# Joining two 256-column weights into one 512-column moving operand in a software-pipelined four-layer graph kernel, with a new hand-written order on every engine

## The chip, the cores and the metric

The kernel runs on one core of one Trainium2 chip. The metric is device time in microseconds (us), from start to end of one execution; the time before is the median of three runs. A core has five engines that work side by side, each through its own list of instructions in the order in which the program wrote them: TensorE (PE: matmuls, which write to PSUM banks; its weight loads, PEld, overlap the matmuls), VectorE (DVE), ScalarE (ACT), GpSimd (POOL) and SyncE (SP, which issues the DMAs). They wait for one another only through semaphores.

## The reference

32 graphs of 256 nodes with 256 features pass through four layers, each with a residual sum and a normalisation (mean and variance over the features). Layers A and D are masked attention with 4 heads of 64, G is a gated graph layer with 4 heads, B an attention with 8 heads of 32 that is also cut by a cosine threshold.

```python
# A, D: attention over the neighbours
attn = softmax(where(adj, q @ k.T / sqrt(64), -big));  y = (attn @ v) @ Wo + bo
# G, h = the node features, for each of 4 heads:
Wh  = h @ W[head].T + bW[head]
A_mat = tanh(where(adj, (Wh @ attn[head]) @ Wh.T, 0))
hp  = relu(A_mat @ Wh)
ha  = concat(hp over heads) @ A_w.T;   hf = h @ fc_w.T
c   = sigmoid(hf @ g1_w.T + ha @ g2_w.T + gbias);   y = hf * c + ha * (1 - c)
# B, 8 heads of 32:
m   = embs @ map_w.T + map_b
n   = m / |m| per head;  cos_adj = (n @ n.T masked) > 0.1
p   = softmax(where(masked, -big, q(m) @ k(m).T / sqrt(32)))
sem_h = embs @ gcn_map_w.T + gcn_map_b;   adj = cos_adj * p
y   = relu((adj @ sem_h) @ gcn_W.T / (adj.sum(-1) + 1))
```

## The kernel before

**Stages and order.** The work on one graph in one layer is cut into stages with names such as `g_wh_0` (layer G, node vectors Wh of head 0), `b_m` (layer B, the product m) or `d_x_t` (layer D, transpose of its input). A step of the program runs one stage list per engine, in which each stage carries the number of steps that its graph lags behind; layers A, G, B and D of up to four graphs are so interleaved. The lists are written out by hand in the tables ORDER (the loop body: 27 iterations, one graph enters and one leaves in each), FILL and DRAIN (ahead of the loop and behind it). Nothing reorders them later: what stands in a table is what the engine does next.

**Products.** float32 values are kept as a high and a low part, and `pe_product` issues three matmuls for each product: high by high, high by low (lines 462 and 463, the same weights) and low by high (464), each with 128 rows of weights and, in the node-major stages, 256 moving columns. `pe_node_major` does so for two halves of the nodes (`it`) and two halves of the features (`kc`): 12 matmuls a stage. `g_wh_h` is one such stage for each of the four heads, into the bank BA[1]; `b_m` and `b_sem` are two more, into BB[1] and BB[0].

**Around the two chains that the prediction speaks of.** In layer B the PE stage `b_out` (line 451, four transposes with `ident,b`) is followed on DVE by `b_scale` (1801), `b_sum` (1805) and `b_stats` (373 and 378), on POOL by `b_rstd` (393 and 395), on DVE by `b_norm_out` (385, two instructions, x from SBUF to SBUF), and then on PE by `d_x_t` (451, `ident,x`). DVE's next stages behind `b_norm_out` are `g_ha_t` (630), for which the PE stage `g_gate` waits, and `g_diff` (1688). While that chain runs PE does the stages `g_ha_h_nt` (six matmuls each), `g_hf`, `g_ha_t` and `g_gate_x`. POOL's stages there are `b_mask` (1882: the uint8 adjacency becomes an additive mask) and `g_x_ha` (1869: a sum of two float32 tiles, all in SBUF). Between A and G the PE stages `b_m`, `b_k`, `b_q` stand ahead of `g_x_t` (451, `ident,a`), which waits for DVE's `a_norm_out` (385); DVE's stage `b_m` (1764, adds the bias) stands just ahead of that. In layer B the PE stages `b_transpose_n` (1420) wait for DVE's `b_cut_n` (1733), which need ACT's `b_exps_n` (1571).

Of the kernel before, what the change touches and what calls it, by code (L numbers as in the profile page):

```python
# [731 lines left out]
def build(nc, d, out_dram):  # L732

    with ExitStack() as ctx:
# [1203 lines left out]
```

## Time and profile before

| | |
|---|---|
| median of 3 runs | 2638.91 us (2637.47 to 2639.14) |
| span of the profiled execution, first to last instruction | 2634.6 us |
| own time of that execution | about 2639 us (its span and some 4 us around it) |
| granted PE clock, mean of the span | 0.989 of full speed |
| PE busy | 2561.4 us, 97% (22,097 matmuls) |
| DVE, ACT, POOL busy | 76%, 54%, 35% |
| loop of 27 iterations | about 334 to 2450 us |

Busy time is the time in which an engine has an instruction in work; matmuls are pipelined, so a matmul's listed duration is longer than the distance to the next one's start, and that distance (the pace) is what counts in a stream. In a row of the timeline the bracket behind an instruction gives how long its engine sat idle ahead of it, and what ended the wait.

### The profile page before, as it was taken

To read this page: it belongs to the slowest core of one execution; us is meant where nothing else is said; L and a number is where in the kernel's file an instruction comes from. 1 tells how busy PE (TensorE), PEld (TensorE's weight loads), DVE (VectorE), ACT (ScalarE), POOL (GpSimd) and SP (SyncE) were. 2 spreads that over 40 slices of the span, in tenths; PEclk is the share of its full clock that TensorE was granted. 3 is DMA by queue.
4 is the path that set the end of the run, shared out by engine and by line. 5 is a ranking of instruction groups with operands and counts; after the bars stand their busy time and mean duration, and the time that the engine had idled before them with its cause. 6 is when DMAs were issued, how large, how long until landed. Compare 5 with 4: busy or idle time off the path is not lost.

```text
span 2634.6 us, 63306 instructions
## 1 busy us (share of the span) xinstructions
PE 2561.4 (97%) x22097; PEld 2293.3 (87%) x22097; DVE 2006.3 (76%) x6629; ACT 1409.9 (54%) x3925; POOL 917.0 (35%) x988
## 2 busy tenths in 40 slices
PE   7999999999999999999999999999999999999985
PEld 7888888898888899888889888889888889888874
DVE  3577877777877787877887787787787787787764
ACT  2355555655654555555565555565565555565442
POOL 3233333343333344333334333334333334433330
PEclk9999999999999999999999999999999999999997
DMA  4000000000000000000000000000000000000000
GB/s 135 7 1 12 11 11 0 10 10 10 10 10 9 1 10 10 10 10 9 1 10 10 10 10 10 0 10 10 10 10 10 4 6 10 10 10 0 11 6 9
DMA packets 44490, 29.90 MB, mean 11 GB/s; under 512 B 21264, under 2 KB 44048, under 8 KB 44432
## 3 DMA queue, kind: packets, MB, share of 16 engines
q1 hardware_dynamic: 44432, 29.13, 3.8%
q8 instruction: 35, 0.57, 0.1%
q14 instruction: 23, 0.19, 0.0%
HBM read 20.73 MB, written 8.39 MB: 11 GB/s over the span
## 4 chain that ended last, share of the span: by engine, by line
PE 84%; ACT 5%; DVE 2%; issue 1%; POOL 0%; ACTq 0%; DVEq 0%; POOLq 0%
PE bank L462 21%; PE bank L464 19%; PE bank L463 19%; PE bank L1420 4%; ACT arena L594 4%; PE bank L519 4%; PE bank L528 3%; PE bank L451 3%; PE bank L1411 3%; PE bank L539 3%; PE bank L1402 2%; PE bank L1430 2%; DVE arena L678 1%; PE bank L1244 1%; DVE b L635 0%
## 5 line engine op out<-in xcount | busy, mean ns | idle before, releaser
L393 POOL TENSOR_SCALAR l_ve<-l_mv 128x2 f32<-128x2 f32 x128 | 28.8, 225 | 1022.2 <-DVE l_mv L378 1021.9
L1571 ACT ACTIVATE b<-b,s_sh 128x256 f32<-128x256 f32 x512 | 254.8, 503 | 97.4 <-DVE s_sh L635 97.4
L462 PE MATMUL bank<-arena_r 128*128 128x256 f32 x1024 | 303.1, 296 | 0.2
L464 PE MATMUL bank<-arena_r 128*128 128x256 f32 x1024 | 289.1, 282 | 0.0
L463 PE MATMUL bank<-arena_r 128*128 128x256 f32 x1024 | 289.0, 282 | 0.0
L1836 POOL TENSOR_TENSOR arena_r<-a,arena_r 128x512 fp32r<-128x512 f32 x128 | 165.5, 1293 | 335.8 <-ACT arena_r L1508 335.7
L1831 POOL TENSOR_TENSOR arena_r<-a,arena_r 128x512 fp32r<-128x512 f32 x128 | 166.7, 1303 | 165.9 <-ACT arena_r L1514 165.9
L1733 DVE SCALAR_TENSOR_TENSOR b<-bank,b 128x256 f32<-128x256 f32 x512 | 191.0, 420 | 36.0 <-ACT b L1571 27.6
L462 PEld LDWEIGHTS bank<-arena_r 128*128 128x128 f32 x1024 | 194.7, 190 | 21.4 <-issue 21.2
L635 DVE CUSTOM_DVE_ANT_0 b<-bank,s_add 128x256 f32<-128x256 f32 x512 | 181.5, 420 | 23.9 <-PE bank L1402 14.8
L463 PEld LDWEIGHTS bank<-arena_r 128*128 128x128 f32 x1024 | 195.2, 191 | 0.0
L464 PEld LDWEIGHTS bank<-arena_r 128*128 128x128 f32 x1024 | 194.8, 190 | 0.0
L1638 DVE SCALAR_TENSOR_TENSOR arena_r<-bank,g_b_z,arena_r 128x256 fp32r<-128x256 f32 x256 | 112.2, 480 | 90.5 <-ACT arena_r L1489 89.6
L594 ACT ACTIVATE b<-b,l_sh 128x256 f32<-128x256 f32 x256 | 126.7, 497 | 85.0 <-DVE l_sh L635 85.0
L462 PE MATMUL bank<-g_w_a_hi,arena_r 128*128 128x256 f32 x512 | 155.0, 303 | 0.0
L462 PE MATMUL bank<-g_w_t_hi,arena_r 128*128 128x256 f32 x512 | 150.8, 295 | 1.5 <-DVE arena_r L630 1.5
L462 PE MATMUL bank<-arena_r,g_w_z_hi 128*128 128x256 f32 x512 | 147.0, 287 | 1.6 <-DVE arena_r L630 1.6
L463 PE MATMUL bank<-arena_r,g_w_z_hi 128*128 128x256 f32 x512 | 143.8, 281 | 0.0
L464 PE MATMUL bank<-arena_r,g_w_z_lo 128*128 128x256 f32 x512 | 143.7, 281 | 0.0
L464 PE MATMUL bank<-g_w_a_hi,arena_r 128*128 128x256 f32 x512 | 143.0, 279 | 0.0
L463 PE MATMUL bank<-g_w_t_lo,arena_r 128*128 128x256 f32 x512 | 142.9, 279 | 0.0
L464 PE MATMUL bank<-g_w_t_hi,arena_r 128*128 128x256 f32 x512 | 142.9, 279 | 0.0
(280 smaller groups left out, 9041.7 us busy)
## 6 DMA issues: line engine op xcount, KB each, us to landing
x_in<-in_x SPq DMA_DIRECT2D x32, 256.0 KB, 2.8
out<-x SPq DMA_DIRECT2D x32, 256.0 KB, 2.1
adj_a<-in_adj SPq DMA_DIRECT2D x32, 64.0 KB, 2.5
adj_b<-in_adj SPq DMA_DIRECT2D x32, 64.0 KB, 1.8
a<-in_L_gnn_W SPq DMA_DIRECT2D x4, 256.0 KB, 3.3
b<-in_L_gnn_A_w SPq DMA_DIRECT2D x1, 1024.0 KB, 7.6
arena<-in_L_gnn_attn SPq DMA_DIRECT2D x4, 256.0 KB, 7.2
g_b_wh<-in_L_gnn_bW SPq DMA_DIRECT2D x1, 512.0 KB, 9.2
```

The source lines that it names most:

```text
L462: pe.matmul(out, w[0], x[0], start=first, stop=False)
L463: pe.matmul(out, w[0], x[1], start=False, stop=False)
L464: return pe.matmul(out, w[1], x[0], start=False, stop=last)
L519: last = pe.matmul(B[2 * pair + half][:, it * NODES:(it + 1) * NODES], L.qt[rows, pair, it * P:(it + 1) * P], L.kt[rows, pair, :], start=T ...
L594: last = act.activation(L.e[:, h, it, :], L.e[:, h, it, :], ACT.Exp, bias=L.sh[:, h, it:it + 1], scale=-1.0, accum_out=L.sums[:, h, it:it ...
L635: return dve.tensor_tensor_reduce(out, scores, add, -scale, ceiling, ALU.add, ALU.min, lowest)
L1420: last = pe.transpose(BB[n][:, jt * NODES + it * P:jt * NODES + (it + 1) * P], S.e[:, n, it, jt * P:(jt + 1) * P], C.ident[:, :])
L1571: last = act.activation(S.e[:, n, it, :], S.e[:, n, it, :], ACT.Exp, bias=S.sh[:, it, h:h + 1], scale=-1.0, accum_out=S.sums[:, it, h:h + 1])
L1638: last = dve.scalar_tensor_tensor(G.zt[h % 2][1][:, dt, :], BA[0][:, dt * NODES:(dt + 1) * NODES], G.b_z[:, dt, h:h + 1], G.zt[h % 2][0][: ...
L1733: last = dve.scalar_tensor_tensor(S.e[:, n, it, :], BB[n][:, it * NODES:(it + 1) * NODES], COS_MIN, S.e[:, n, it, :], ALU.is_gt, ALU.mult, ...
L1831: pool.tensor_tensor(G.wh[h % 2][1], G.whf[:, h % 2, :, :], G.wh[h % 2][0].bitcast(F32), ALU.subtract).then_inc(G.wh_sb.sem, 1)
L1836: pool.tensor_tensor(G.am[h % 2][1], G.th[:, h % 2, :, :], G.am[h % 2][0].bitcast(F32), ALU.subtract).then_inc(G.a.sem, 1)
```

## The change

The weights of two heads of `g_wh` are kept side by side (`G.w_t_pair`, 512 columns), and so are those of `b_m` and `b_sem` (`S.w_ms`). A new helper, `pe_node_rows`, multiplies one half of the nodes by all 512 columns and fills a whole bank: the stage `g_wh_h` now computes node half h % 2 for the head pair h // 2, with 6 matmuls of 512 columns for 12 of 256; `b_m` computes m and sem for both node halves, with 12 of 512 for 24 of 256, into BB[0] and BB[1], and PE's stage `b_sem` is gone. DVE adds the bias to the two heads in one instruction of 512 elements for each `g_wh` stage. ACT's and POOL's parts of head 0 now need both stages of the pair. Some waits are added (PE's `b_m` for `D.o_sb`, `b_unit_t` for `S.sem_sb`; ACT's `g_a` for `G.p_psum`; two of SP's loads). All tables are written anew; the loop body also begins at another stage.

```diff
+def pe_node_rows(pe, out, x_t, w, it):
+
+    for kc in range(T):
+        last = pe_product(pe, out, part(x_t, slice(None), kc, slice(it * P, (it + 1) * P)), part(w, slice(None), kc),
+                          kc == 0, kc == T - 1)
+    return last
...
-                pe_node_major(pe, BA[1], G.xt, G.w_t[h]).then_inc(G.wh_psum.sem, 1)
+                pe_node_rows(pe, BA[1][:, :], G.xt, G.w_t_pair[h // 2], h % 2).then_inc(G.wh_psum.sem, 1)
...
-                pe_node_major(pe, BB[1], S.xt, S.w_m).then_inc(S.m_psum.sem, 1)
+                    pe.wait_ge(D.o_sb.sem, D.o_sb.all(g - 1))
+                for it in range(T):
+                    last = pe_node_rows(pe, BB[it][:, :], S.xt, S.w_ms, it)
+                last.then_inc(S.m_psum.sem, 1)
...
-            def b_sem(g):
-                pe.wait_ge(S.x_t_sb.sem, S.x_t_sb.at(g))
-                if later(g):
-                    pe.wait_ge(D.o_sb.sem, D.o_sb.all(g - 1))
-                pe_node_major(pe, BB[0], S.xt, S.w_s).then_inc(S.sem_psum.sem, 1)
...
             def b_unit_t(g):
                 pe.wait_ge(S.unit.sem, S.unit.at(g))
+                pe.wait_ge(S.sem_sb.sem, S.sem_sb.at(g))
...
             def g_wh(g, h):
-                act.wait_ge(G.wh_f.sem, G.wh_f.at(g, h + 1))
+                act.wait_ge(G.wh_f.sem, G.wh_f.at(g, h - h % 2 + 2))
...
             def g_wh(g, h):
+                pair, it = h // 2, h % 2
                 dve.wait_ge(G.wh_psum.sem, G.wh_psum.at(g, h + 1))
-                if h >= 2:
-                    dve.wait_ge(G.wh_sb.sem, G.wh_sb.at(g, h - 1))
-                for it in range(T):
-                    last = dve.tensor_tensor(G.whf[:, h % 2, it, :], BA[1][:, it * DIM:(it + 1) * DIM],
-                                             G.b_wh[:, h * DIM:(h + 1) * DIM], ALU.add)
-                last.then_inc(G.wh_f.sem, 1)
+                if pair:
+                    dve.wait_ge(G.wh_sb.sem, G.wh_sb.at(g, 2))
+                dve.tensor_tensor(G.whf[:, :, it, :], view(BA[1]),
+                                  G.b_wh[:, 2 * pair * DIM:(2 * pair + 2) * DIM].rearrange("p (h n) -> p h n", n=DIM),
+                                  ALU.add).then_inc(G.wh_f.sem, 1)
```

The tables put other neighbours around these stages. The order of PE in the loop body around `b_out` was this; `g_w_a1` to `g_w_a3` are the weights of the `g_ha` stages, one stage for each change of weights or bank (three rows, then three more), and the row with `b32` is `b_out`:

```order
L464 MATMUL bank2<-g_w_a1_hi,arena_r_50 128x256
L1435 ISA
L451 MATMUL bank4<-ident,b32 128x128 x4
L462 MATMUL bank2<-g_w_a2_hi,arena_r_50 128x256
L463 MATMUL bank2<-g_w_a2_lo,arena_r_50 128x256
L464 MATMUL bank2<-g_w_a2_hi,arena_r_50 128x256
```

and is now this, still on PE:

```order
L465 MATMUL bank2<-g_w_a1_hi,arena_r_50 128x256
L1452 REGISTER_ALU
L452 MATMUL bank4<-ident,b32 128x128 x4
L463 MATMUL bank2<-g_w_a3_hi,arena_r_50 128x256
L464 MATMUL bank2<-g_w_a3_lo,arena_r_50 128x256
L465 MATMUL bank2<-g_w_a3_hi,arena_r_50 128x256
```

The stage `g_ha_2_1` (weights `g_w_a2`) stood behind `b_out` and stands two stages ahead of it now: behind `b_out` come `g_ha_3_1`, `g_ha_3_0`, `g_hf`, `g_ha_t`, `g_gate_x`, `d_x_t` and `g_gate`, as before but for that one. On POOL the rows from `b_sums` (`s_sd`) on, with `b_rstd` (`l2_ve`, `l2_rs`), were these:

```order
L1901 TENSOR_TENSOR s_sd<-s_sums,s_drop 128x16
L393 TENSOR_SCALAR l2_ve<-l2_mv 128x2
L395 TENSOR_TENSOR l2_rs<-l2_ve,minus_half 128x2
L1878 ISA
L1882 TENSOR_SCALAR s_add<-adj_b 128x512
L1869 TENSOR_TENSOR a32<-a32 128x512
L728 TENSOR_TENSOR x3<-x3,l3_bo 128x256 x2
```

and are now, on POOL again:

```order
L394 TENSOR_SCALAR l2_ve<-l2_mv 128x2
L396 TENSOR_TENSOR l2_rs<-l2_ve,minus_half 128x2
L1882 REGISTER_ALU
L1886 TENSOR_TENSOR a32<-a32 128x512
L1870 ISA
L1874 CAST g_adj_bf<-adj_a 128x512
L742 TENSOR_TENSOR a32<-x_in,l0_bo 128x256 x2
L742 TENSOR_TENSOR x3<-x3,l3_bo 128x256 x2
```

`g_x_ha` (`a32<-a32`) stands right behind `b_rstd` where `b_mask` (`s_add`) stood; six stages now stand between `b_rstd` and `b_mask`. On DVE the rows around the first `b_cut` (`b,s_dsum<-bank,b`) were these, at the end of the loop body before:

```order
L1647 TENSOR_TENSOR a<-a,g_adj_t 128x512
L1638 SCALAR_TENSOR_TENSOR arena_r<-bank,g_b_z,arena_r 128x256 x2
L1731 ISA
L1733 SCALAR_TENSOR_TENSOR b,s_dsum<-bank,b 128x256 x2
L1731 REGISTER_ALU
L1733 SCALAR_TENSOR_TENSOR b,s_dsum<-bank,b 128x256 x2
```

and are now, on DVE, where the row `x<-x,l_mv,l_rs` is `d_norm_out`:

```order
L1655 SCALAR_TENSOR_TENSOR arena_r<-bank,g_b_z,arena_r 128x256 x2
L1748 ISA
L1750 SCALAR_TENSOR_TENSOR b,s_dsum<-bank,b 128x256 x2
L386 TENSOR_SCALAR x<-x,l_mv,l_rs 128x256 x2
L1748 REGISTER_ALU
L1750 SCALAR_TENSOR_TENSOR b,s_dsum<-bank,b 128x256 x2
```

`d_norm_out` moved from a place ahead of all four masks to one between the first two cuts. In the same table `g_c_t` and `g_z_1` moved behind `b_mask_0`, and `g_diff` moved ahead of `b_norm_out`. On PE `b_k` moved from between `b_m` and `b_q` to a place behind `g_x_t`.

## Rows read from the trace of the kernel before

**Rows 1.** The page: head and first line of the busy times (its part 1).

```profile
span 2634.6 us, 63306 instructions
PE 2561.4 (97%) x22097; PEld 2293.3 (87%) x22097; DVE 2006.3 (76%) x6629; ACT 1409.9 (54%) x3925; POOL 917.0 (35%) x988
```

**Rows 2.** Busy time by stretch; columns named in the first line.

```profile
core 0: us, PE busy (x) PEld busy (x) DVE busy (x) ACT busy (x) POOL busy (x), PEclk, DMA share, GB/s
330.00:2450.00 2120.00, 2110.21 (x18456) 1892.42 (x18459) 1678.49 (x5575) 1178.59 (x3301) 759.96 (x812) 1.00 0.03 8
76.00:81.00 5.00, 4.91 (x23) 4.58 (x24) 1.10 (x4) 1.30 (x3) 0.00 (x0) 0.50 0.00 0
```

**Rows 3.** Timeline (start, duration, engine, line, instruction, [idle before]) of DVE, one iteration apart.

```profile
1277.40 0.69 DVE L1801 TENSOR_TENSOR x<-bank,s_fac 128x512 f32<-128x512 f32 x1 [1.85 <-PE bank L451]
...
1355.76 0.69 DVE L1801 TENSOR_TENSOR x<-bank,s_fac 128x512 f32<-128x512 f32 x1 [1.85 <-PE bank L451]
```

**Rows 4.** Timeline of PE: from `b_m` to `g_x_t`, first matmul of each stage.

```profile
1231.71 0.28 PE L462 MATMUL bank<-s_w_m_hi,b32r 128*128 128x256 f32 x1
...
1233.13 0.28 PE L462 MATMUL bank<-b32r,s_w_k_hi 128*128 128x256 f32 x1
...
1234.58 0.28 PE L462 MATMUL bank<-b32r,s_w_q_hi 128*128 128x256 f32 x1
...
1236.01 0.60 PE L451 MATMUL bank<-ident,a 128*128 128x128 f32 x4
```

**Rows 5.** Timeline of PE in the fill, two neighbours of a `g_wh` stage.

```profile
80.10 0.41 PE L464 MATMUL bank<-g_w_t_hi,arena_r 128*128 128x256 f32 x1
80.31 0.41 PE L462 MATMUL bank<-g_w_t_hi,arena_r 128*128 128x256 f32 x1
```

**Rows 6.** Timeline of PE: `b_out`, the two `g_ha` stages behind it, `d_x_t`, `g_gate`.

```profile
1276.65 0.60 PE L451 MATMUL bank<-ident,b 128*128 128x128 f32 x4
...
1277.80 0.28 PE L462 MATMUL bank<-g_w_a_hi,arena_r 128*128 128x256 f32 x1
...
1278.50 0.28 PE L462 MATMUL bank<-g_w_a_hi,arena_r 128*128 128x256 f32 x1
...
1282.48 0.60 PE L451 MATMUL bank<-ident,x 128*128 128x128 f32 x4
1282.97 0.39 PE L462 MATMUL bank<-g_w_g_hi,arena_r 128*128 128x256 f32 x1
```

**Rows 7.** Timeline of DVE in that stretch: `b_norm_out`, `g_ha_t`.

```profile
1281.19 1.13 DVE L385 TENSOR_SCALAR x<-x,l_mv,l_rs 128x256 f32<-128x256 f32 x2 [1.24 <-POOL l_rs L395]
1282.24 0.68 DVE L630 TENSOR_TENSOR arena_r<-bank,arena_r 128x512 fp32r<-128x512 f32 x1
```

**Rows 8.** Timeline of POOL in that stretch: `b_mask`, `g_x_ha`.

```profile
1281.24 1.54 POOL L1882 TENSOR_SCALAR s_add<-adj_b 128x512 bf16<-128x512 uint8 x1
1282.76 1.28 POOL L1869 TENSOR_TENSOR a<-a 128x512 f32<-128x512 f32 x1
```

**Rows 9.** Timelines of DVE and POOL at one `d_norm_out`, near the loop's end.

```profile
2445.19 1.71 DVE L385 TENSOR_SCALAR x<-x,l_mv,l_rs 128x256 f32<-128x256 f32 x2
...
2444.07 1.30 POOL L1836 TENSOR_TENSOR arena_r<-a,arena_r 128x512 fp32r<-128x512 f32 x1 [2.28 <-ACT arena_r L1508]
2445.33 1.43 POOL L1831 TENSOR_TENSOR arena_r<-a,arena_r 128x512 fp32r<-128x512 f32 x1
```

**Rows 10.** Timeline of DVE: bias add of `b_m`, then `a_norm_out`.

```profile
1233.72 0.72 DVE L1764 TENSOR_TENSOR b<-bank,s_b_m 128x256 f32<-128x256 f32 x2
1235.03 0.74 DVE L385 TENSOR_SCALAR a<-a,l_mv,l_rs 128x256 f32<-128x256 f32 x2 [0.59 <-POOL l_rs L395]
```

**Rows 11.** Timelines of DVE (`d_norm_out`, end of the last of four cuts) and PE (`b_transpose_2`, `_3`).

```profile
1243.32 0.73 DVE L385 TENSOR_SCALAR x<-x,l_mv,l_rs 128x256 f32<-128x256 f32 x2
...
1256.67 0.42 DVE L1733 SCALAR_TENSOR_TENSOR b<-bank,b 128x256 f32<-128x256 f32 x1
...
1256.97 1.03 PE L1420 MATMUL bank<-ident,b 128*128 128x128 f32 x8
```

More of the change, by code:

```diff
@@ L110 @@
-        ("a_q", 1), ("a_v", 1), ("a_scores_0", 1), ("b_x_t", 0), ("a_scores_1", 1), ("b_m", 0), ("b_k", 0),
-        ("a_probs_0", 1), ("a_probs_1", 1), ("a_probs_2", 1), ("a_probs_3", 1), ("a_values_0", 1), ("a_values_1", 1),
-        ("b_q", 0), ("a_out", 1), ("b_sem", 0), ("g_adj_t", 1), ("b_unit_t", 0), ("b_scores_0", 0), ("g_x_t", 1),
[7 rows of a table removed]
-        ("g_ha_t", 1), ("a_x_t", 2), ("d_q", 0), ("g_gate_x", 1), ("d_scores_0", 0), ("g_gate", 1), ("d_v", 0),
[3 rows of a table removed]
-        ("a_out", 2), ("d_out", 0), ("b_sem", 1), ("b_m", 1), ("g_x_t", 2), ("b_q", 1), ("b_k", 1), ("g_c", 2),
[7 rows of a table removed]
@@ new lines @@
+        ("a_q", 1), ("a_v", 1), ("b_x_t", 0), ("a_scores_0", 1), ("a_scores_1", 1), ("b_q", 0), ("b_m", 0),
+        ("a_probs_0", 1), ("a_probs_1", 1), ("a_probs_2", 1), ("a_probs_3", 1), ("a_values_0", 1), ("a_values_1", 1),
+        ("b_k", 0), ("a_out", 1), ("b_unit_t", 0), ("g_x_t", 1), ("b_scores_0", 0), ("g_adj_t", 1), ("g_wh_0", 1),
[6 rows of a table added]
+        ("g_ha_3_1", 1), ("g_hf", 1), ("d_x_t", 0), ("g_ha_t", 1), ("a_x_t", 2), ("g_gate_x", 1), ("g_gate", 1),
+        ("d_k", 0), ("d_q", 0), ("d_v", 0), ("a_k", 2), ("d_scores_0", 0), ("d_scores_1", 0), ("a_q", 2), ("a_v", 2),
@@ L144 @@
+        ("g_gate", 2), ("d_q", 1), ("d_k", 1),
     ],
@@ L182 @@
-        ("b_stats", 0), ("g_p_3", 1), ("b_norm_out", 0), ("d_x_t", 0), ("g_diff", 1), ("a_x_t", 2), ("g_ha_t", 1),
-        ("d_mask_0", 0), ("g_gate", 1), ("d_mask_1", 0), ("d_v", 0), ("g_mix", 1), ("g_sum", 1), ("d_norm_p_0", 0),
[3 rows of a table removed]
-        ("b_x_t", 1), ("a_sum", 2), ("a_stats", 2), ("d_sum", 0), ("a_norm_out", 2), ("b_m", 1), ("b_square", 1),
-        ("g_x_t", 2), ("b_sem", 1), ("d_stats", 0), ("b_unit", 1), ("g_z_0", 2), ("g_c_t", 2), ("g_wh_0", 2),
-        ("g_adj_t", 2), ("g_z_1", 2), ("b_mask_0", 1), ("b_mask_1", 1), ("b_mask_2", 1), ("b_mask_3", 1),
@@ new lines @@
+        ("g_z_3", 0), ("g_wh_3", 0), ("g_p_1", 0), ("g_a_3", 0), ("g_p_2", 0), ("g_p_3", 0), ("g_ha_t", 0),
+        ("g_diff", 0), ("g_gate", 0), ("a_x_t", 1), ("g_mix", 0), ("g_sum", 0), ("g_stats", 0), ("g_norm_out", 0),
+        ("a_v", 1), ("b_x_t", 0), ("a_mask_0", 1), ("a_mask_1", 1), ("a_mask_2", 1), ("a_mask_3", 1),
+        ("a_norm_p_0", 1), ("a_norm_p_1", 1), ("a_probs_1", 1), ("a_probs_3", 1), ("b_m", 0), ("b_square", 0),
+        ("a_o_copy", 1), ("b_sem", 0), ("a_sum", 1), ("a_stats", 1), ("b_unit", 0), ("a_norm_out", 1), ("g_x_t", 1),
[6 rows of a table added]
@@ L191 @@
+        ("b_stats", 0), ("g_p_3", 1), ("b_norm_out", 0), ("g_diff", 1), ("g_ha_t", 1), ("a_x_t", 2), ("d_x_t", 0),
+        ("g_gate", 1), ("g_mix", 1), ("g_sum", 1), ("g_stats", 1), ("d_v", 0), ("d_mask_0", 0), ("d_mask_1", 0),
[3 rows of a table added]
+        ("d_sum", 0), ("b_x_t", 1), ("a_sum", 2), ("a_stats", 2), ("b_m", 1), ("a_norm_out", 2), ("b_square", 1),
+        ("g_x_t", 2), ("d_stats", 0), ("g_adj_t", 2), ("b_sem", 1), ("g_wh_0", 2), ("b_unit", 1), ("g_z_0", 2),
[4 rows of a table added]
     ],
     "POOL": [
-        ("b_keep", 0), ("a_bias", 0), ("a_mask", 0), ("g_adj", 0), ("d_mask", 0), ("w_d", 0), ("a_rstd", 0),
@@ L221 @@
-        ("b_m", 0), ("b_sem", 0), ("b_k", 0), ("b_q", 0), ("b_unit_t", 0), ("b_scores_0", 0), ("b_cos_0", 0),
-        ("b_transpose_0", 0), ("b_transpose_1", 0), ("b_transpose_2", 0), ("b_transpose_3", 0), ("b_values_0", 0),
-        ("b_scores_1", 0), ("b_cos_1", 0), ("b_transpose_4", 0), ("b_transpose_5", 0), ("b_transpose_6", 0),
-        ("b_transpose_7", 0), ("b_values_1", 0), ("b_out", 0), ("d_x_t", 0), ("d_q", 0), ("d_k", 0), ("d_v", 0),
-        ("d_scores_0", 0), ("d_scores_1", 0), ("d_probs_0", 0), ("d_probs_1", 0), ("d_probs_2", 0), ("d_probs_3", 0),
@@ new lines @@
+        ("g_x_t", 1), ("g_wh_0", 1), ("b_sem", 2), ("b_unit", 2), ("g_c_t", 1), ("g_z_0", 1), ("g_z_1", 1),
[5 rows of a table added]
+        ("b_copy_7", 2), ("g_p_3", 1), ("b_factors", 2), ("b_scale", 2), ("b_sum", 2), ("b_stats", 2), ("g_diff", 1),
+        ("b_norm_out", 2), ("g_ha_t", 1), ("d_x_t", 2), ("g_gate", 1), ("g_mix", 1), ("g_sum", 1), ("g_stats", 1),
[3 rows of a table added]
+        ("a_probs_1", 0), ("a_probs_3", 0), ("d_o_copy", 2), ("b_x_t", 1), ("a_o_copy", 0), ("d_sum", 2),
+        ("d_stats", 2), ("a_sum", 0), ("a_stats", 0), ("b_m", 1), ("a_norm_out", 0), ("b_square", 1), ("g_x_t", 0),
```

207 lines of the change are left out of this document (108 added, 99 removed), and 225 rows, old and new, of tables (DRAIN, FILL, ORDER).

## The prediction, made before the changed kernel was run

> **What bounds the kernel now.** I read the page first. PE is busy for 2561.4 of 2634.6 us [rows 1], so the question is whether the stream of matmuls ever stops. The busy times by stretch answer it: in the loop PE is busy for 2110.21 of 2120.00 us, at a granted clock of 1.00, which is the 2.4 GHz level [rows 2]. The loop is bound by PE; DVE and the others set the time only where PE reaches an instruction before its input is there. The timeline gives the period: the same DVE instruction comes again after 78.36 us [rows 3], and 27 iterations make some 2,115 us. So each 0.1 us that PE gains or loses in an iteration is 2.7 us at the end, and 0.2% (5.3 us), about what a measurement of this kernel can tell from no change, is 0.2 us an iteration.
>
> The sum is made against the profiled execution's own time, about 2639 us, which is the median of the runs to within a microsecond.
>
> **Term 1, the wide matmuls.** Per graph, four `g_wh` stages lose 6 matmuls each and `b_m` with `b_sem` loses 12: 36 pairs of 256 columns become 36 matmuls of 512, with the same columns in all. At full clock 12 matmuls of `b_m` take 1.42 us, from 1231.71 to 1233.13 [rows 4], 118 ns each; over the `g_wh` stages it is 114 to 118, and I take 117.5, so a pair costs 235 ns. The trace has no 512-column matmul of this kind, so it is bounded. At the half clock (0.50, the 1.2 GHz level [rows 2]) the same 256 columns come every 210 ns [rows 5], a column a cycle and nothing more. The upper bound is therefore twice today's pace, 235 ns, no gain; the lower is 512 columns at 2.4 GHz, 213 ns. If the 10 ns that today's pace has over 107 are paid once an instruction it is 224. Since nothing of the surcharge shows at the half clock, I take 219: 36 x 16 ns = **0.58 us saved** per graph, between 0 and 0.77.
>
> The Trainium skill, "TensorE: Matmul & The Clock Gate", section "Back-to-back issue gap", prices an isolated matmul at 109 ns for 256 columns and 216 for 512. The trace disagrees with its first figure (118). By both its figures the saving would be 36 x 2.5 ns, 0.09 us a graph; with its second figure and the row it would be 0.7. The same section gives 131 ns for 512 columns in a sustained stream; by that the saving would be 36 x 104 ns, 3.7 us a graph, and with the terms below the kernel would take about 2566 us. Rows 5 speak against it, since there the time follows the columns.
>
> PE is the bound, so this gain counts in full, if no new wait eats it. DVE's four saved instructions a graph count for nothing: DVE is busy for 79% of the loop [rows 2] and PE does not wait for its bias adds; they are hidden under PE's other stages.
>
> **Term 2, `b_out` to `g_gate`.** This place decides. From `b_out`'s end DVE and POOL run a fixed chain: scale, sum, statistics, POOL's `b_rstd`, `b_norm_out`, then `g_ha_t`; PE does other work meanwhile. Today the chain and the cover end together: PE starts `d_x_t` at 1282.48 and `g_gate` at 1282.97 [rows 6], and DVE ends `b_norm_out` at 1282.32 and `g_ha_t` at 1282.92 [rows 7]. PE's cover has about 0.1 us to spare at `d_x_t` and none at `g_gate`. In the change one `g_ha` stage, 0.70 us (1277.80 to 1278.50 [rows 6]), stands ahead of `b_out` instead of behind it. The chain is not shortened: `g_diff` moves ahead of `b_norm_out`, into DVE's idle 1.24 us there [rows 7], but `g_ha_t` still stands behind `b_norm_out`. So `g_gate` starts as long after `b_out` as before, with 0.70 us less work in between: **+0.70 us**. The stage that moved ahead covers nothing there, for PE did not wait at `b_out`.
>
> Then the chain may grow. `b_norm_out` takes 1.13 us for two instructions while POOL's `b_mask` starts 0.05 us behind it [rows 7, 8]; the same two instructions take 0.73 to 0.74 elsewhere [rows 10, 11]. One `d_norm_out` took 1.71: it began at 2445.19, POOL's sum of two SBUF tiles at 2445.33, and DVE's pair ended about when POOL did, at 2446.76 to 2446.90 [rows 9]. In the change POOL's instruction right behind `b_rstd` is `g_x_ha`, of the kind of rows 9 and 1.28 us long [rows 8]; it needs `g_ha`, long done by then. Its start falls against `b_norm_out` as in rows 9: first instruction 0.4 us, second held until POOL ends, 0.05 + 1.28 + 0.4 = 1.73 us or less. Bounds are 0.73 (no contact, -0.40 against today) and 1.73 (+0.60); I take 1.69, by the row it is nearest to: **+0.56**.
>
> The Trainium skill, "SBUF — State Buffer", section "🔬 SBUF: two separate sides", says that DVE and GpSimd share a port pair as an exclusive lock, held by whichever starts first for its whole instruction. Rows 9 agree for two-input sums; `b_mask` cost 0.40 rather than its whole 1.54.
>
> **Term 3, `g_x_t`.** PE reaches `g_x_t` 4.30 us behind the start of `b_m` today [rows 4], 0.24 after `a_norm_out` ends (1235.77 [rows 10]), of which some 0.05 is the signal. In the change the wide `b_m` (12 x 0.219 = 2.63) and `b_q` (1.43 [rows 4]) stand ahead: 4.06. But DVE's bias add for `b_m` is queued ahead of `a_norm_out` and now waits for the whole wide stage: 1231.71 + 2.63 + 0.1 for the signal + 0.72 = 1235.16, then `a_norm_out` to 1235.90, while PE is there at 1235.77. **+0.2 us**, between 0.1 and 0.3.
>
> **Term 4, the first four transposes.** `b_transpose_2` starts at 1256.97 and `_3` some 0.4 later, the last cut ends at 1257.09 [rows 11]: 0.25 us to spare. The change puts `d_norm_out` (0.73 [rows 11]) and two gated-layer stages between `b_mask_0` and the last cut, where DVE has idle time but no more than about as much. PE's distance from `b_scores_0` to these transposes is the same (`g_s_2` came ahead of them, `g_p_0` went behind). Between nothing and 0.5; I take **+0.25**.
>
> The moved `b_k`, `a_v` and `d_probs` lie beside work that does not wait for them; the added waits are for stages that end a layer earlier: nothing. The two SP waits hold the adjacency loads until the masks are made, one graph ahead of use: nothing either.
>
> **Sum** per iteration: -0.58 + 0.70 + 0.56 + 0.2 + 0.25 = **+1.13 us**, times 27: +30.5. In the fill and drain five graphs save 3 us and meet the same neighbours at `b_out`, about as much again: 0. Forecast **2670 us**; own range 2655 to 2685.
>
> **The rivals.**
> *`g_x_ha` does not meet `b_norm_out`* (it starts late, or DVE's pair goes first): the stretch stays at 1.13. For it: `b_mask` starts at the same point and costs only 0.40. Against: rows 9. -0.58 + 0.70 + 0.2 + 0.25 = 0.57, 2654 us. 0.22.
> *Faster.* `b_norm_out` at its bare 0.73, because `b_mask` is gone from its side, and wide matmuls near 215 ns (-0.72): term 2 falls to 0.30, terms 3 and 4 to 0.1 each: -0.22, 2633 us. The point that decides is `b_norm_out` below 0.9 us. For it: 0.73 wherever POOL is quiet. Against: POOL is not quiet there. 0.15.
> *`d_norm_out` is held as well.* It now sits among cuts, where POOL runs its two-input sums back to back, as in rows 9: 1 us more against 0.25 to spare, +0.75 on the forecast, 2690 us. For it: just such a place in rows 9. Against: DVE's idle time ahead of the cuts may absorb it. 0.15.
> *Columns faster than one a cycle*: 131 ns a wide matmul, -3.74 + 1.71 an iteration, 27 times, and five graphs of -3.7 outside the loop: 2566 us. Rows 5 speak against it; 0.01. It is the sustained figure of the Trainium skill quoted above.
>
> **How the numbers follow.** The forecast has 0.47. Range 2636 to 2693: it takes in the second rival's case and the third's and leaves out most of the faster one. Faster: 0.15 and 0.01 make 0.16; within 0.2%: the edge between the no-contact case and the faster one, 0.05; slower 0.79.
>
> **What would show it.** Wide matmuls starting every 219 ns (213 to 235); `g_gate`'s first matmul idle 0.7 us or more, released by `g_ha_t` on DVE; `b_norm_out` near 1.7 us beside a 1.28 us `g_x_ha`; `g_x_t` idle 0.2 behind `a_norm_out`; `b_transpose` idle behind a cut; a period near 79.5 us. I am wrong if the period is below 78.4, above all if PE does not wait at `g_gate` although a stage less covers the chain, or if `b_norm_out` is short.

## The result and the profile after

The changed kernel takes 2715.57 us (median of 4 runs, 2712.48 to 2716.89) against 2638.68 before: a ratio of 1.0297, 95% interval 1.0285 to 1.0309. It is 77 us slower; the forecast was 2670 and the range ended at 2693. The profiled execution has a span of 2714.4 us, 79.8 more than [rows 1]. That is 3 us more than the medians differ by: wherever a run here lists both, an execution takes some 1.9 us more than its span, so the profiled execution of before took about 2636.5 us, 2 us under the median, and not the 2639 that the prediction set its sum against.

The page of the changed kernel, its head and first line of busy times:

```profile
span 2714.4 us, 60943 instructions
PE 2592.9 (96%) x20945; PEld 2235.0 (82%) x20945; DVE 2015.2 (74%) x6501; ACT 1411.5 (52%) x3925; POOL 919.0 (34%) x988
```

There are 1152 matmuls fewer, 36 for each of 32 graphs, and PE is busy for 31.5 us *more*: a matmul counts to its modelled end, so busy time is not work done. The busy times by stretch of the changed kernel (columns as in [rows 2]) show it in the loop's steady part:

```profile
350.00:2440.00 2090.00, 2038.36 (x16701) 1756.60 (x16700) 1613.38 (x5231) 1129.30 (x3161) 733.01 (x780) 1.00 0.03 8
```

PE now stands idle for 2.5% of it, at the same granted clock; before it was 0.5% [rows 2]. The timeline of DVE in the changed kernel gives the period, 80.73 us for 78.36 [rows 3]:

```profile
1317.41 0.69 DVE L1818 TENSOR_TENSOR x<-bank,s_fac 128x512 f32<-128x512 f32 x1 [1.85 <-PE bank L452]
...
1398.14 0.69 DVE L1818 TENSOR_TENSOR x<-bank,s_fac 128x512 f32<-128x512 f32 x1 [1.84 <-PE bank L452]
```

The loop and its ends (the fill ahead of it, the drain behind it) can be taken apart. `b_out` of the second graph starts at 258.54 us before and 266.43 after; 27 graphs later it starts at 2373.42 and 2447.79. So the 27 periods cost 66.5 us, 2.46 each; the fill cost 7.9 and the drain 5.4.

To see which stage the 2.46 us are in, I took the distance from each PE stage's first matmul to that of the next stage, as the median over 17 graphs of the loop. They sum to 78.38 us before and 80.81 after. These are the stages that changed by over 0.2 us, with the two that stand behind such a one or lost matmuls (`d_x_t`, `g_wh`) and with `b_sem`, which is gone. A wait counts for the stage ahead of it:

```
stage (next stage)                 before   after
g_gate_x (d_x_t)                     1.50    2.95
d_x_t (g_gate)                       0.50    0.60
b_m and b_sem                        2.94    2.81
b_q (after: g_x_t)                   1.44    1.65
b_transpose_1 (after: _2)            0.36    0.79
b_transpose_2 (_3)                   0.43    0.69
a_probs_1                            0.98    0.47
d_values_0                           0.91    1.42
g_wh_0 to g_wh_3, sum                5.95    5.91
```

The wait at `a_probs_1` only moved to `d_values_0`. What is left of the loop's 2.43 us is +1.56 at `d_x_t` and `g_gate`, +0.28 at `g_x_t` (0.06 of it in the next stage), +0.74 at the transposes (0.06 in the third), -0.17 from the wide matmuls: 2.41 in all.

**The place at `d_x_t`.** In this place PE covers a chain on DVE and POOL: it does other work (the cover) while the chain runs, and waits if the cover ends first. The waits of PE for a normalisation (`x`) and for the cuts (`b`), as the profile sums them, for the kernel before and then for the changed one (us in total, times, longest):

```profile
PE bank L451 <- DVE x L385: 4.6, 1, 4.6
PE bank L1420 <- DVE b L1733: 2.1, 3, 0.9
```

```profile
PE bank L452 <- DVE x L386: 42.8, 31, 4.6
PE bank L1437 <- DVE b L1750: 7.4, 31, 0.9
```

One wait for a normalisation became 31, and three for the cuts became 31. The timelines of PE, DVE and POOL of the changed kernel, where [rows 6 to 8] stood:

```profile
1323.24 0.66 PE L452 MATMUL bank<-ident,x 128*128 128x128 f32 x4 [1.30 <-DVE x L386]
1323.84 0.39 PE L463 MATMUL bank<-g_w_g_hi,arena_r 128*128 128x256 f32 x1
```

```profile
1321.20 1.99 DVE L386 TENSOR_SCALAR x<-x,l_mv,l_rs 128x256 f32<-128x256 f32 x2 [0.31 <-POOL l_rs L396]
1323.10 0.68 DVE L644 TENSOR_TENSOR arena_r<-bank,arena_r 128x512 fp32r<-128x512 f32 x1
```

```profile
1321.14 1.27 POOL L1886 TENSOR_TENSOR a<-a 128x512 f32<-128x512 f32 x1
1322.37 0.67 POOL L1874 CAST g_adj_bf<-adj_a 128x512 bf16<-128x512 uint8 x1
```

`b_norm_out` starts 3.79 us behind `b_scale`, exactly as before (1281.19 - 1277.40), and then takes 1.99 us for 1.13. Its two instructions took 1.37 and 0.69 us. POOL's `g_x_ha` started 0.06 us ahead of it.

**The wide matmuls.** Two neighbours in `b_m` of the changed kernel at the full clock, then two in the fill at the granted clock 0.50:

```profile
1270.16 0.39 PE L463 MATMUL bank<-s_w_ms_hi,b32r 128*128 128x512 f32 x1
1270.39 0.39 PE L464 MATMUL bank<-s_w_ms_lo,b32r 128*128 128x512 f32 x1
...
1272.97 0.28 PE L463 MATMUL bank<-b32r,s_w_q_hi 128*128 128x256 f32 x1
```

```profile
145.86 0.63 PE L463 MATMUL bank<-g_w_t_hi,arena_r 128*128 128x512 f32 x1
146.28 0.63 PE L464 MATMUL bank<-g_w_t_lo,arena_r 128*128 128x512 f32 x1
```

Twelve take 2.81 us, 234 ns each, at the full clock: twice the 118 of [rows 4]. At the half clock they come every 420 to 430 ns, twice [rows 5].

**The ends.** Busy times by stretch, for the kernel before (fill up to the second `b_out`, drain behind the 29th) and then for the changed one, whose last row lies in its fill (PEclk is the third figure from the end):

```profile
0.00:258.50 258.50, 234.77 (x1869) 212.86 (x1870) 154.11 (x468) 114.89 (x295) 86.35 (x97) 0.97 0.14 40
2373.40:2634.60 261.20, 221.52 (x1816) 192.23 (x1814) 177.45 (x599) 118.87 (x336) 70.94 (x79) 0.92 0.02 7
```

```profile
0.00:266.40 266.40, 241.78 (x1779) 212.39 (x1780) 154.43 (x456) 114.75 (x295) 84.86 (x96) 0.94 0.13 38
2447.80:2714.40 266.60, 223.57 (x1726) 188.00 (x1724) 177.65 (x591) 119.14 (x336) 69.11 (x79) 0.91 0.02 7
140.40:147.20 6.80, 6.20 (x31) 4.50 (x32) 4.08 (x19) 0.82 (x2) 0.00 (x0) 0.50 0.00 0
```

Length times mean granted clock is 250.7 us before and 250.4 after in the fill, 240.3 and 242.6 in the drain. So, by this estimate (good to about 1.3 us each, as the clock is rounded), the 7.9 us of the fill are time at the half clock, and so are some 3 of the drain's 5.4. Where the row at 0.50 begins, PE waits twice in the changed fill:

```profile
139.33 0.66 PE L452 MATMUL bank<-ident,b 128*128 128x128 f32 x4 [2.57 <-DVE b L1790]
141.00 1.12 PE L452 MATMUL bank<-ident,a 128*128 128x128 f32 x4 [1.01 <-DVE a L386]
```

All eleven traces with the fill of the changed kernel have that 2.57 us wait, and in all of them the granted clock falls to 0.50 during it or within 2 us behind it; before, the mean clock from 90 us to the second `b_out` is 1.00. Not all of the 7.9 us belongs to the change: the run below with the old fill (`e13_before_pool`) reached its second `b_out` at 261.58 us, at a mean clock of 0.95.

### The profile page after: what moved, and what is told of

The parts are those of the page before. It is cut to its first block, busy times and chain, and to the rows that moved or that the text cites. A ratio compares the mean times of both kernels' runs of the same rounds, so it can differ in the third digit from the quotient of the medians.

```text
span 2714.4 us, 60943 instructions
## 1 busy us (share of the span) xinstructions
PE 2592.9 (96%) x20945; PEld 2235.0 (82%) x20945; DVE 2015.2 (74%) x6501; ACT 1411.5 (52%) x3925; POOL 919.0 (34%) x988
## 4 chain that ended last, share of the span: by engine, by line
PE 80%; DVE 13%; issue 3%; POOL 1%; ACT 1%; DVEq 0%; DMA 0%; POOLq 0%; SPq 0%; ACTq 0%
PE bank L463 18%; PE bank L465 16%; PE bank L464 16%; PE bank L533 5%; PE bank L542 4%; PE bank L553 4%; PE bank L1437 4%; PE bank L452 4%; DVE x L386 3%; PE bank L1428 3%; PE bank L1419 2%; PE bank L1447 2%; DVE b L1750 2%; DVE l_st L374 1%; DVE arena L649 1%
## 5 line engine op out<-in xcount | busy, mean ns | idle before, releaser
L1848 POOL TENSOR_TENSOR arena_r<-a,arena_r 128x512 fp32r<-128x512 f32 x128 | 166.3, 1300 | 443.8 <-ACT arena_r L1531 441.6
L1853 POOL TENSOR_TENSOR arena_r<-a,arena_r 128x512 fp32r<-128x512 f32 x128 | 177.0, 1383 | 148.9 <-ACT arena_r L1525 148.9
L463 PE MATMUL bank<-g_w_a_hi,arena_r 128*128 128x256 f32 x512 | 154.9, 303 | 0.1
L1437 PE MATMUL bank<-ident,b 128*128 128x128 f32 x1024 | 144.0, 280 | 8.3 <-DVE b L1750 7.4
L1517 ACT ACTIVATE a<-bank,g_c 128x256 f32<-128x256 f32 x256 | 106.8, 471 | 82.6 <-PE bank L465 82.4
L1664 DVE TENSOR_TENSOR a<-a,g_adj_t 128x512 f32<-128x512 f32 x128 | 105.4, 824 | 51.7 <-ACT a L1517 51.5
L1504 ACT ACTIVATE arena_r<-bank,g_b_z 128x256 fp32r<-128x256 f32 x256 | 107.1, 472 | 70.2 <-PE bank L465 70.1
```

Source lines behind the costliest of these rows:

```text
L463: pe.matmul(out, w[0], x[0], start=first, stop=False)
L1437: last = pe.transpose(BB[n][:, jt * NODES + it * P:jt * NODES + (it + 1) * P], S.e[:, n, it, jt * P:(jt + 1) * P], C.ident[:, :])
L1848: pool.tensor_tensor(G.wh[h % 2][1], G.whf[:, h % 2, :, :], G.wh[h % 2][0].bitcast(F32), ALU.subtract).then_inc(G.wh_sb.sem, 1)
L1853: pool.tensor_tensor(G.am[h % 2][1], G.th[:, h % 2, :, :], G.am[h % 2][0].bitcast(F32), ALU.subtract).then_inc(G.a.sem, 1)
```

## The experiments

All moves are in the loop's table ORDER alone, on the changed kernel if nothing else is said; `...` marks what is left out of an edit. Times are medians of four or five runs, ratios against the kernel before, timed again beside each group of runs (medians 2633.8 to 2638.7 us).

### The place at `d_x_t`: POOL's neighbour, PE's cover

```diff
-("b_rstd", 3), ("g_x_ha", 2), ("g_adj", 1),
+("b_rstd", 3), ("b_mask", 2), ("g_x_ha", 2), ("g_adj", 1),
...
-("g_rstd", 2), ("b_mask", 2), ("a_rstd", 1),
+("g_rstd", 2), ("a_rstd", 1),
```

> The changed kernel with one move: POOL's b_mask stands right behind b_rstd again and g_x_ha behind it, in the loop only. Theory held: in the changed kernel g_x_ha (two tiles in SBUF, 1.27 us) and the cast behind it hold b_norm_out at 1.99 us, and all of that is on the path to d_x_t. Then b_norm_out falls to about 1.13 us as beside b_mask before the change, PE's wait at d_x_t falls from 1.30 to about 0.45, the period from 80.8 to about 79.95, and the time from 2715.6 to about 2692 us. Rival: the lost cover alone makes the wait and POOL's neighbour does not matter; then nothing changes, 2715 us.

2693.11 us, 1.0206 (1.0189 to 1.0223): 22 us less than the changed kernel. The timelines of DVE and POOL:

```profile
1311.86 1.13 DVE L386 TENSOR_SCALAR x<-x,l_mv,l_rs 128x256 f32<-128x256 f32 x2 [0.31 <-POOL l_rs L396]
```

```profile
1311.91 1.54 POOL L1899 TENSOR_SCALAR s_add<-adj_b 128x512 bf16<-128x512 uint8 x1
```

The only stage of PE that changed by over 0.05 us is `g_gate_x`, with the wait ahead of `d_x_t`: -0.85 us. The rival falls.

```diff
-("b_values_1", 2), ("g_ha_2_1", 1), ("g_ha_1_1", 1), ("b_out", 2), ("g_ha_3_1", 1),
+("b_values_1", 2), ("g_ha_1_1", 1), ("b_out", 2), ("g_ha_2_1", 1), ("g_ha_3_1", 1),
```

> The changed kernel with one move: PE's g_ha_2_1 (0.71 us) stands behind b_out again instead of two stages ahead of it, in the loop only. Theory held: the chain from b_out over DVE and POOL to d_x_t is of fixed length and PE only covers it, so 0.71 us more cover takes 0.71 us from the wait at d_x_t (1.30 to about 0.6) and 27 times that from the time: about 2696 us. Rival: the chain starts later by as much as the cover grows, since something else than b_out starts it; then nothing changes, 2715 us.

2694.14 us, 1.0215 (1.0198 to 1.0232), 21 us less; that wait shrank by 0.69 us, and the period is 80.03.

> Both moves together: b_mask behind b_rstd, and g_ha_2_1 behind b_out. Theory held: the two add up, the wait at d_x_t goes (1.30 and the 0.1 of the restart), period about 79.3, time about 2676 us. Rival: with the one gone the other was not needed, or g_gate waits for g_ha_t next; then the gain is no more than that of the better one alone, about 2692 us.

2672.83 us, 1.0137 (1.012 to 1.0154): 43 us less, the sum of the two; period 79.13, `g_gate_x` at 1.50 and `d_x_t` at 0.50 as before the change. So this place is two causes that add up. The last test is the other way round, on the kernel before:

```diff
-("b_rstd", 3), ("b_mask", 2), ("g_x_ha", 2), ("d_bias", 3),
+("b_rstd", 3), ("g_x_ha", 2), ("b_mask", 2), ("d_bias", 3),
```

> The kernel before the change with one move: POOL's g_x_ha stands right behind b_rstd and b_mask behind it, the neighbours of the changed kernel. Theory held: b_norm_out grows from 1.13 to about 2.0 us, PE has 0.1 us to spare at d_x_t and waits for the other 0.75, the period is 79.1 us and the time 2638 + 27 x 0.75, about 2658 us. Rival: the long b_norm_out belongs to the changed kernel's other order (g_diff ahead of it, the cast behind g_x_ha); then about 2638 us.

2664.59 us, 1.0098 (1.008 to 1.0117). The timelines of DVE and POOL:

```profile
1296.73 2.07 DVE L385 TENSOR_SCALAR x<-x,l_mv,l_rs 128x256 f32<-128x256 f32 x2 [1.23 <-POOL l_rs L395]
```

```profile
1296.67 1.29 POOL L1869 TENSOR_TENSOR a<-a 128x512 f32<-128x512 f32 x1
1298.05 1.50 POOL L1882 TENSOR_SCALAR s_add<-adj_b 128x512 bf16<-128x512 uint8 x1
```

One exchange of two neighbours on an engine that is busy for 35% costs 26 us: the period grew by 0.92 us, more than expected, since `b_norm_out` itself grew by 0.94.

### The transposes: who is late

```diff
-("b_mask_2", 2), ("g_a_0", 1), ("b_mask_3", 2),
+("b_mask_2", 2), ("d_norm_out", 3), ("g_a_0", 1), ("b_mask_3", 2),
...
-("b_cut_0", 2), ("d_norm_out", 3), ("b_cut_1", 2), ("g_a_1", 1), ("b_cut_2", 2),
+("b_cut_0", 2), ("b_cut_1", 2), ("g_a_1", 1), ("b_cut_2", 2),
```

> The changed kernel with one move: DVE's d_norm_out (0.73 us) stands behind b_mask_2 in DVE's idle time instead of between the first two cuts, in the loop only. Theory held: it delays the cuts, and PE's third and fourth transposes wait for them (0.43 and 0.25 us more than before the change): most of 0.7 us an iteration comes back, time about 2697 us. Rival: the cuts are late because g_a_1, which stands among them, is held by POOL (1.13 us for 0.69) and because b_cos came a stage later; then no more than 0.3 us an iteration comes back, about 2708 us or more.

2714.18 us, 1.0284 (1.0267 to 1.0301): no time came back that could be measured, where the theory had 18 us and the rival up to 8. The changed kernel's DVE and POOL, then this run's:

```profile
1292.75 0.73 DVE L386 TENSOR_SCALAR x<-x,l_mv,l_rs 128x256 f32<-128x256 f32 x2
...
1294.09 1.13 DVE L1664 TENSOR_TENSOR a<-a,g_adj_t 128x512 f32<-128x512 f32 x1
```

```profile
1293.37 1.31 POOL L1848 TENSOR_TENSOR arena_r<-a,arena_r 128x512 fp32r<-128x512 f32 x1 [5.76 <-ACT arena_r L1531]
1294.63 1.74 POOL L1853 TENSOR_TENSOR arena_r<-a,arena_r 128x512 fp32r<-128x512 f32 x1
```

```profile
1295.38 1.76 DVE L1664 TENSOR_TENSOR a<-a,g_adj_t 128x512 f32<-128x512 f32 x1
1297.07 0.41 DVE L1750 SCALAR_TENSOR_TENSOR b<-bank,b 128x256 f32<-128x256 f32 x1
```

```profile
1295.30 1.30 POOL L1848 TENSOR_TENSOR arena_r<-a,arena_r 128x512 fp32r<-128x512 f32 x1 [5.75 <-ACT arena_r L1531]
```

Without `d_norm_out` ahead of it `g_a_1` (line 1664) starts earlier and takes 0.63 us longer: it ends some 0.5 us behind POOL's sum whenever it starts. The cuts queue behind it.

```diff
-("b_cut_1", 2), ("g_a_1", 1), ("b_cut_2", 2), ("b_cut_3", 2), ("b_copy_1", 2),
+("b_cut_1", 2), ("b_cut_2", 2), ("b_cut_3", 2), ("g_a_1", 1), ("b_copy_1", 2),
```

> The changed kernel with one move: DVE's g_a_1 stands behind b_cut_3 instead of ahead of b_cut_2, in the loop only. Theory held after the move of d_norm_out gave nothing: g_a_1 ends at the same time whenever it starts, since it is held until POOL's sum of two tiles in SBUF ends (it took 1.13 us in the changed kernel and 1.76 when it started earlier), and cuts 2 and 3 queue behind it. Without it ahead of them PE's third and fourth transposes come 0.6 to 0.7 us an iteration earlier: about 2698 us. Rival: ACT's b_exps_2 and _3, which come late too, hold the cuts; then no more than 0.3 us comes back, 2708 us or more.

2712.37 us, 1.0287 (1.0271 to 1.0302). The transposes did come 0.50 us earlier, where 0.6 to 0.7 were expected; but the next stage that needs DVE, `b_values_0`, now waits 0.47 us, for the copies (`b_copy_3`) that queue behind `g_a_1` and `g_wh_2`. This run's waits of PE:

```profile
PE bank L1447 <- DVE b L1759: 12.9, 29, 0.9
```

In the changed kernel that wait is 1.8 us in all. So both stages were put behind the copies, with the two moves at `d_x_t` made as well:

```diff
-("b_cut_1", 2), ("g_a_1", 1), ("b_cut_2", 2), ("b_cut_3", 2),
-("b_copy_1", 2), ("g_wh_2", 1), ("b_copy_3", 2), ("g_a_2", 1),
+("b_cut_1", 2), ("b_cut_2", 2), ("b_cut_3", 2),
+("b_copy_1", 2), ("b_copy_3", 2), ("g_wh_2", 1), ("g_a_1", 1), ("g_a_2", 1),
```

> The changed kernel with three groups of moves in the loop: b_mask behind b_rstd (POOL), g_ha_2_1 behind b_out (PE), and g_wh_2 and g_a_1 behind both copies of the first transposes (DVE). a_norm_out, b_m and g_x_t stay where the change put them. Theory held: the wait at the transposes (0.5 us) is one of its own and comes back without a new one, so the period is 79.12 - 0.54, about 78.6 us, and the time about 2658 us, less than the run with a_norm_out moved too (2665). What then stays over before is 0.28 us at g_x_t less 0.17 us from the wide matmuls, and fill and drain. Rival: at this place too the wait only moves on (to b_values_0 or g_p_1): 2668 us or more.

2659.94 us, 1.0089 (1.0072 to 1.0106), the fastest version with wide matmuls; period 78.66, 0.47 less than with the two moves at `d_x_t` alone. The wait is one of its own, and taking what queues on DVE between the cuts and the copies out of the way gives back 0.52 us of the 0.74. The other 0.22 stay; 0.08 of them are no wait, since `b_transpose_1` now has a transpose behind it instead of a product, and that takes 0.43 or 0.44 us instead of 0.36.

### What the wide matmuls are worth

```diff
+    for n in range(2):
+        for kc in range(T):
+            last = pe_product(pe, out[:, n * DIM:(n + 1) * DIM], part(x_t, slice(None), kc, slice(it * P, (it + 1) * P)),
+                              part(w, slice(None), kc, slice(n * DIM, (n + 1) * DIM)), kc == 0, kc == T - 1)
-    for kc in range(T):
-        last = pe_product(pe, out, part(x_t, slice(None), kc, slice(it * P, (it + 1) * P)), part(w, slice(None), kc),
-                          kc == 0, kc == T - 1)
```

> The changed kernel with each 512-column matmul issued as two of 256 columns, all else the same (also the order, the banks and DVE's 512-element adds). Theory held: the pace above one column a cycle is paid by the column, not by the instruction, so 36 wide matmuls are worth what the trace shows, 0.17 us an iteration: about 2720 us. Rival, the price in the prediction (16 ns saved a pair, 0.58 us a graph): about 2734 us. Rival with 11 ns an instruction: 2728 us.

2717.62 us, 1.0311 (1.0295 to 1.0326). The period is 0.04 us above the changed kernel's as the mean of 27 (80.83 against 80.79) and 0.07 by the sum of its stages: 1 to 2 ns for each of the 36 matmuls. The price in the prediction is out, and so is 11 ns an instruction.

### What stands between `g_x_t` and `g_wh_0`

The next run has the tables of before with wide matmuls. Two of the edits in the loop:

```diff
-("g_adj_t", 0), ("b_sem", 1), ("g_wh_0", 0),
+("g_adj_t", 0), ("g_wh_0", 0),
...
-("g_a_1", 2), ("g_wh_2", 2), ("b_copy_2", 3),
+("g_a_1", 2), ("b_copy_2", 3),
...
-("g_a_2", 2), ("b_exps_4", 3),
+("g_a_2", 2), ("g_wh_2", 2), ("b_exps_4", 3),
```

> The wide matmuls and their waits with the order tables of before, all three of them; only b_sem leaves PE's list, and the stages of head 0 and head 2 on ACT and POOL (g_wh_0, g_wh_2) and two on DVE and POOL move back where they would otherwise wait for a stage behind them. Theory held: nearly all of the 77 us is the new order and not the wide matmuls; these alone bring 0.17 us an iteration and 5 to 6 us in all, time about 2633 us (2628 to 2642). Rival: joining two heads makes the stages of the first head wait for the second and brings waits of its own; then 2650 us or more.

2699.83 us, 1.0237 (1.0223 to 1.0251). My theory fell: the wide matmuls cost 63 us even in the old order. In the loop it is one wait; the period is 79.60, and this run's waits of PE show 29 waits at a matmul for DVE's `g_x_t` (line 643 here):

```profile
PE bank L462 <- DVE arena_r L643: 37.1, 29, 1.6
```

Before, `b_sem` (1.51 us) stood between `g_adj_t` and `g_wh_0` and covered ACT's and DVE's work on the transposed input. The merged stage stands ahead of `g_x_t`, and the cover is gone: +1.44 us an iteration. The changed kernel has `b_k` there. Some 30 us of this run are fill and drain, where the same cover is missing and nothing was put in its place; that was read from the trace, not tested. The mean granted clock is lower there than before as well (0.94 in the fill, 0.91 in the drain), which makes some 12 of these 30 us by the estimate above.

Two more moves on top of that run:

```diff
-("b_m", 1), ("b_k", 1), ("b_q", 1), ("g_x_t", 0), ("g_adj_t", 0), ("g_wh_0", 0),
+("b_m", 1), ("b_q", 1), ("g_x_t", 0), ("g_adj_t", 0), ("b_k", 1), ("g_wh_0", 0),
...
-("b_m", 2), ("a_norm_out", 1), ("b_square", 2), ("g_x_t", 1),
+("a_norm_out", 1), ("b_m", 2), ("b_square", 2), ("g_x_t", 1),
```

> The run with the order of before and wide matmuls, with two moves in the loop: PE's b_k stands behind g_adj_t, where b_sem stood before, and DVE's a_norm_out stands ahead of b_m's bias add. Theory held: what the wide matmuls cost in the old order is the cover that b_sem gave between g_x_t and g_wh_0 (1.44 us an iteration); with b_k as cover and a_norm_out not held by the wide b_m the period falls from 79.6 to about 78.2 us, that of before less the 0.17 us that wide matmuls save, and the time from 2700 to about 2662 us, the rest being fill and drain, which are left as they were. Rival: g_x_t now comes before a_norm_out is ready and the wait only moves there: period 78.6 or more, 2672 us or more.

2669.44 us, 1.0132 (1.0114 to 1.0151), period 78.69: of the 1.44 us 0.91 came back with the cover. The rest, 0.51 us, is a wait at `g_wh_0`, since DVE's `g_x_t` now stands behind the late bias add. The rival was right that a wait is left, and wrong on its place.

The same was seen on the changed kernel in three runs. With the moves of the first runs, `g_a_1` behind `b_cut_3`, and `b_k` ahead of `g_x_t`:

```diff
-("b_m", 2), ("b_q", 2), ("g_x_t", 1), ("g_adj_t", 1), ("b_k", 2), ("g_wh_0", 1),
+("b_m", 2), ("b_q", 2), ("b_k", 2), ("g_x_t", 1), ("g_adj_t", 1), ("g_wh_0", 1),
```

> The changed kernel with four moves in the loop together: b_mask behind b_rstd (POOL), g_ha_2_1 behind b_out (PE), g_a_1 behind b_cut_3 (DVE), b_k ahead of g_x_t (PE). Theory held: the waits are separate and add up, 1.56 us at d_x_t, 0.65 at the transposes, 0.28 at g_x_t: 27 x 2.5 us less, about 2648 us, the period that of before the change or 0.1 us below; what stays above before is the fill and the drain (13 us). Rival: one wait hid another (PE comes earlier and meets a wait that was covered, at a_probs or d_values above all); then 2660 us or more.

2703.67 us, 1.0255 (1.0239 to 1.0271), not 2648: the wait at `g_x_t` went (0.28 us) and one of 1.44 at `g_wh_0` came; the 0.47 us at `b_values_0` came too, as in the run with `g_a_1` moved alone. With the moves of the first runs, `b_k` left in place, `a_norm_out` ahead of the bias add, and `g_wh_2` and `g_a_1` behind the copies:

```diff
-("b_m", 2), ("a_norm_out", 1), ("b_square", 2), ("g_x_t", 1),
+("a_norm_out", 1), ("b_m", 2), ("b_square", 2), ("g_x_t", 1),
```

> The changed kernel with moves in the loop alone: b_mask behind b_rstd (POOL), g_ha_2_1 behind b_out (PE), a_norm_out ahead of b_m's bias add (DVE), and g_wh_2 and g_a_1 behind both of DVE's copies of the first transposes. b_k stays behind g_x_t, since the run with it ahead of g_x_t showed PE waiting 1.44 us at g_wh_0 for the node vectors' input. Theory held: the lost time in the loop is three waits of PE that the new order made (1.56 us at d_x_t, 0.28 at g_x_t, 0.74 at the transposes with the copies behind them); with all gone the period is 78.2 us, 0.15 below before, and the time about 2646 us, of which 13 us are fill and drain. Rival: a stage moved back on DVE becomes late for PE in its turn (g_a_1 for g_p_1, or b_m for the unit vectors): 2655 us or more.

2665.36 us, 1.011 (1.0093 to 1.0127); period 78.85, 0.42 us of it new at `g_wh_0`. With DVE's `g_x_t` ahead of `b_square` as well:

```diff
-("a_norm_out", 1), ("b_m", 2), ("b_square", 2), ("g_x_t", 1),
+("a_norm_out", 1), ("b_m", 2), ("g_x_t", 1), ("b_square", 2),
```

> The run before (five moves in the loop) with one more: DVE's g_x_t stands ahead of b_square. Theory held: there PE's g_wh_0 waited 0.42 us an iteration for DVE's g_x_t, which b_m's bias add and b_square, moved behind a_norm_out, had pushed back; with b_square out of its way the period falls from 78.86 to about 78.45 us and the time from 2665 to about 2654 us, still above before. Rival: ACT's part of g_x_t is what comes late; then nothing changes, 2665 us.

2709.16 us, 1.0264 (1.0238 to 1.0291), a clear miss: the 0.42 us went, but `b_square` starts the chain to the unit vectors over POOL's 2.9 us, and PE waits 1.36 us behind `b_unit_t` and 0.55 ahead of it (waits of PE):

```profile
PE bank L463 <- DVE arena_r L1655: 32.7, 27, 1.2
PE bank L452 <- DVE b L1790: 16.7, 29, 3.6
```

In this run alone the granted clock also falls to 0.50 inside the loop: five short stretches are at it, the first from 1280.6 us on, 1 us behind such waits of 0.38 and 1.21 us. So its time is not the price of the wait alone.

Three stages need DVE there, `a_norm_out`, `g_x_t` and `b_square`, and `m` comes 1.4 us later. Each of the three orders tried has a wait; 0.28 us, the change's own choice, is the least of them. That no other order does better is not shown.

## Why the prediction was wrong

The sign and the places of three of the waits were right, the sizes were not; the range ended 23 us short. By its own steps, for one iteration:

**Term 1, forecast -0.58, measured -0.17** (stage sums), or -0.04 to -0.07 by the run with narrow matmuls. The step that failed is "I take 219" for a wide matmul: it took 234, next to the upper bound of 235. The reason given, that nothing of the surcharge shows at the half clock, holds for wide matmuls too and says nothing on whether it goes by the instruction. The measured answer is that at the full clock it goes by the column. The Trainium skill ("TensorE: Matmul & The Clock Gate", "Back-to-back issue gap") has 216 ns for an isolated matmul of 512 columns and 131 in a stream; both differ from the 234 here, and the measurement decides.

**Term 2, forecast +1.26, measured +1.56.** The lost cover was right (0.70; the run that put it back gained 0.69), though PE waits at `d_x_t`, not at `g_gate`. The second half was mis-sized: `b_norm_out` at 1.69, measured 1.99. The step that failed is "first instruction 0.4 us, second held": that is how [rows 9] went, where DVE came 0.14 us ahead of the sum that held it (the sum before that, 2444.07 to 2445.37, was within 0.2 us of its end). Here `b_rstd` releases DVE while POOL simply goes on, so POOL starts 0.06 us ahead, and both instructions are long: 1.37 us for the first, which ends 0.16 behind POOL's sum, and 0.69 for the second, beside the cast. The run on the kernel before showed the same (2.07). The Trainium skill ("SBUF — State Buffer", "🔬 SBUF: two separate sides") says that whichever of VectorE and GpSimd starts first holds the port pair that they share for its whole instruction. The sums of two tiles agree with it (1.99 and 2.07 us, and 1.76 for `g_a_1`); beside `b_mask`, 1.54 us long, the pair took 1.13, so there it was not held to the end.

**Term 3, forecast +0.2, measured +0.28.** Right. What the prediction did not see is why `b_k` had moved: its clause "lie beside work that does not wait for them" is wrong for `b_k`, which replaces `b_sem` as the cover of `g_wh_0`.

**Term 4, forecast +0.25, measured +0.74.** The place was right and the cause wrong. Moving `d_norm_out` away gave nothing back; moving `g_a_1` and `g_wh_2` gave 0.52. The step that failed is to count PE's distance from `b_scores_0`. From there to the third transpose it is the same indeed (11.86 us before, 11.83 in the fastest run above, medians over the loop), but `b_scores_0` feeds ACT's `b_exps`, and the cuts also need `b_cos_0`. In the page of before and then of the changed kernel DVE idles ahead of the cuts for the one and then for the other:

```profile
L1733 DVE SCALAR_TENSOR_TENSOR b<-bank,b 128x256 f32<-128x256 f32 x512 | 191.0, 420 | 36.0 <-ACT b L1571 27.6
L1750 DVE SCALAR_TENSOR_TENSOR b<-bank,b 128x256 f32<-128x256 f32 x512 | 188.0, 419 | 30.3 <-PE bank L1428 23.0
```

`b_cos_0` (line 1428) now comes a stage (`g_s_1`) later. From its start to the third transpose PE has 4.87 us of work in the fastest run and had 6.34 before, so that what queues on DVE among the cuts is no longer covered. `g_a_1` stood among them before as well, and was held there too (0.92 us). No run put `b_cos_0` back, so this step is argued from the two traces and not tested.

**Fill and drain, forecast 0, measured 13.3.** The prediction took the same neighbours for the same waits and left the granted clock out. By the estimate from the rows above some 11 of the 13.3 us are time at the half clock; some 3 of them came in a run with the old fill as well. No run moved a stage in the fill or the drain, so which move there makes the waits of PE is open.

The misses in us: 0.41 + 0.30 + 0.08 + 0.49 = 1.28 an iteration, 27 times 35, and 13 for the ends: 48, against 46 between the forecast and the median. The third rival's size (2690) was nearer than the forecast, by another mechanism.

## What to carry to other kernels

Before two matmul stages are merged to save instructions, price an instruction by the column at the clock that the kernel runs at: here half the instructions of these stages were worth 0.04 to 0.17 us of 78. Then ask what each of the two stages covered where it stood, and when its consumers now get their input; the merged stage gives both results at its end. And in a kernel whose chains end together with their cover, the neighbour of a VectorE operation on GpSimd is part of the schedule: one exchange of two GpSimd instructions, with nothing else changed, cost 1%.
